# A macaron transformer layer on one core: the opening's transposes, norms and weight halves in another order

## The reference, cut to what matters

```
x = x + 0.5 * ffn(layernorm(x))          # W = dequant(q, scales, zeros) + lora; 512 x 512, and a bias
x = x + block(layernorm(x))              # below
x = x + 0.5 * ffn(layernorm(x))          # the same W

def block(h):                            # res = h
    h = res + mamba2(rmsnorm(h))         # w_in 512 -> 1284, causal conv of 4 taps, silu, scan by chunks of 128, w_out
    return h + mlp(rmsnorm(h))           # silu(gate) * up, 1792 wide, down
```

## Time and profile before

| | |
|---|---|
| median of 3 runs | 748.85 us (748.61 to 750.54) |
| the profiled execution | 749.22 us, its span 747.5 us |
| TensorE busy | 737.0 us, 99% of the span |
| VectorE busy | 637.2 us, 85% |
| ScalarE busy | 455.7 us, 61% |
| GpSimd busy | 341.5 us, 46% |

### The profile page before, as it was taken

How to read it: one execution, slowest core, us unless ns; L and a number is a source line. 1 busy time by engine, 2 the same in 40 slices (tenths; PEclk the granted TensorE clock), 3 DMA queues, 4 the chain that set the end, 5 groups by cost and what they waited for, 6 DMA issues and landing times.

```text
span 747.5 us, 10693 instructions
## 1 busy us (share of the span) xinstructions
PE 737.0 (99%) x3443; PEld 362.0 (48%) x3443; DVE 637.2 (85%) x1254; ACT 455.7 (61%) x895; POOL 341.5 (46%) x393
## 2 busy tenths in 40 slices
PE   9999999999999999989999999999999999999998
PEld 4454455555555565534444444444444444444444
DVE  7899999889989997977999977977977977767994
ACT  4977888687887777435446555456457356444441
POOL 5731446665453457896232153143243242214574
PEclk9999999999999999999999999999999999999999
DMA  8934646574431224320703635635634734434465
GB/s 301 217 76 82 163 96 126 121 134 100 100 85 43 44 71 121 77 84 1 170 14 60 153 59 99 153 57 94 159 57 85 168 58 77 78 71 84 114 169 141
DMA packets 98886, 77.83 MB, mean 104 GB/s; under 512 B 65616, under 2 KB 73104, under 8 KB 98832
## 3 DMA queue, kind: packets, MB, share of 16 engines
q0 software_dynamic: 17280, 31.46, 23.7%
q1 hardware_dynamic: 78640, 41.09, 21.3%
q10 hardware_dynamic: 2912, 4.61, 2.1%
HBM read 24.94 MB, written 5.54 MB: 41 GB/s over the span
## 4 chain that ended last, share of the span: by engine, by line
PE 73%; DVE 16%; ACT 4%; DMA 3%; issue 2%; POOL 1%; SPq 0%; ACTq 0%; DVEq 0%; POOLq 0%
PE PS L2285 61%; DVE stage L1672 2%; PE PS L2431 1%; DMA raw_d<-down_t 1%; PE PS L2423 1%; DVE st L1495 1%; PE PS L2389 1%; PE PS L2416 1%; PE PS L2420 1%; PE PS L2399 1%; DVE raw L1672 1%; PE PS L2407 1%; PE PS L2381 1%; PE PS L2529 1%; DVE h2n_p L1585 1%
## 5 line engine op out<-in xcount | busy, mean ns | idle before, releaser
L2285 PE MATMUL PS<-h,w_in 128*128 128x512 f16 (+1 forms) x504 | 108.1, 369 | 0.0
L2285 PE MATMUL PS<-h,x_t 128*128 128x512 f16 x408 | 95.5, 384 | 2.9 <-DMA h<-h2n_p 2.9
L784 POOL DMA_DIRECT2D xs<-x x42 | 36.7, 882 | 91.7 <-ACT x L1361 88.6
L2285 PEld LDWEIGHTS PS<-h,w_in 128*128 128x128 f16 x504 | 48.8, 98 | 59.9 <-issue 11.0
L2285 PE MATMUL PS<-n_T,stage 128*128 128x512 f16 x288 | 71.5, 379 | 0.0
L2285 PEld LDWEIGHTS PS<-h,x_t 128*128 128x128 f16 x408 | 39.7, 99 | 52.6 <-issue 4.5
L1361 ACT ACTIVATE x<-PS,d_d 128x512 f32<-128x512 f32 x59 | 40.3, 683 | 38.7 <-PE PS L2285 38.7
L584 POOL TENSOR_TENSOR r<-mv,mhalf 128x1 f32<-128x1 f32 (+1 forms) x32 | 29.0, 905 | 50.2 <-DVE mv L1499 36.4
L1331 ACT ACTIVATE xds<-tm,dgh 128x512 f32<-128x512 f32 x24 | 17.3, 722 | 53.4 <-DVE tm L2209 53.4
L2285 PE MATMUL PS<-pre,stage 128*128 128x512 f16 x192 | 49.3, 379 | 0.0
L2285 PEld LDWEIGHTS PS<-n_T,stage 128*128 128x128 f16 x288 | 28.1, 98 | 34.0 <-ACT x L1361 0.3
(11 more groups left out here) (346 smaller groups left out, 1880.6 us busy)
## 6 DMA issues: line engine op xcount, KB each, us to landing
xs<-x POOLq DMA_DIRECT2D x58, 256.0 KB, 3.3
xs<-n POOLq DMA_DIRECT2D x21, 256.0 KB, 3.3
xl<-x POOLq DMA_DIRECT2D x17, 256.0 KB, 3.3
x_t<-x_in SPq DMA_DIRECT2D x16, 256.0 KB, 4.0
x_t<-hb POOLq DMA_DIRECT2D x16, 256.0 KB, 4.8
out<-x_t SPq DMA_DIRECT2D x15, 256.0 KB, 2.3
raw_gu<-gate_t SPq DMA_DIRECT2D x7, 512.0 KB, 4.5
raw_gu<-up_t SPq DMA_DIRECT2D x7, 512.0 KB, 6.5
```

The source lines that it names most:

```text
L784: po.dma_start(end_row(c), d_tmps[d % 3], accum_op=ALU.add).then_inc(s_acc[d % 3], 16)
L2285: ins = pe.matmul(out_, lhs(a, b, k), rhs(a, b, k), start=first and n == 0, stop=last and n == len(todo) - 1)
```

## The change

On four engines the order of the opening is changed:

- TensorE: `first_f` can be done in parts. Block 4's transpose stands before the last of the four matmuls of block 3, block 5's behind the second of block 4; the transpose of the second maximum stands behind block 3's product, its spread behind the first matmul of block 4.
- ScalarE: `hi1` is two functions, the whole result (`hi1_whole`) and the high half (`hi1_high`). For blocks 1 and 2 the copy of a transposed block stands between them. `build_dw(0)` is ahead of `tc0(1)`, `w_in_sum(2)` ahead of `tc0(3)` and `hi1(0)`, and `hi1(3)` is behind the first piece of `w_in_hi`.
- VectorE: the low half of block 1 comes after block 5's statistics and the row of the maximum; `both_scales` before `x1_stats(3)`; `w_in_lo(0)` before the low half of block 3 and `x1_stats(4)`.
- GpSimd: `ln1_chain(2)`, `ln0(5)` and the bias DMA of block 4 stand before the selector `sel_f`.

```diff
@@ GpSimd
             ln1_chain(1, 1)
             ln0(4, 0)
+            ln1_chain(2, 2)
+            ln0(5, 1)
+            xb(4, 0)
             chain(po.memset(sel_f[:, :], 0.0))
...
-            ln1_chain(2, 2)
-            xb(4, 0)
             chain(po.tensor_copy(sel_b[:, :], sel_f[:, :]))
             po.sem_inc(e_const, 1)
-            ln0(5, 1)
             ln1_chain(3, 3)
@@ ScalarE
-                for dst in (hn_of(c), hn_parts(c)[:, 0, :]):
-                    last = ac.activation(dst, row(c), ACT.Identity, scale=r1[:, c, 1:2], bias=b1[:, c, 1:2])
-                last.then_inc(e_hn_hi, 1)
+                ac.activation(hn_of(c), row(c), ACT.Identity, scale=r1[:, c, 1:2], bias=b1[:, c, 1:2])
+
+            def hi1_high(c):
+                ac.activation(hn_parts(c)[:, 0, :], row(c), ACT.Identity, scale=r1[:, c, 1:2], bias=b1[:, c, 1:2]).then_inc(e_hn_hi, 1)
...
             hi0(1, 1)
-            tc0(1)
             ac.wait_ge(s_head, 48)
             ac.activation(a_neg[:, :], al[:, :], ACT.Exp).then_inc(e_aexp, 1)
             ac.wait_ge(e_tab, 2)
             build_dw(0)
+            tc0(1)
             hi0(2, 2)
...
             hi0(3, 3)
             w_in_sum(1)
+            w_in_sum(2)
             tc0(3)
             hi1(0, 0)
-            w_in_sum(2)
             w_in_sum(3)
-            hi1(1, 1)
             hi0(4, 0)
+            hi1_whole(1)
             tc0(4)
-            hi1(2, 2)
+            hi1_high(1)
             hi0(5, 1)
-            hi1(3, 3)
+            hi1_whole(2)
             tc0(5)
+            hi1_high(2)
             ac.wait_ge(e_scale, 1)
             w_in_hi(W_IN_PIECES[0])
+            hi1(3, 3)
             w_in_hi(W_IN_PIECES[1])
@@ VectorE
             x1_stats(2, 2, B_P[0])
             w_in_bound()
-            lo1(1, 1)
             prep0(5, 1)
             max_row(1)
+            lo1(1, 1)
+            both_scales()
             x1_stats(3, 3, B_P[1])
-            both_scales()
             lo1(2, 2)
+            w_in_lo(0)
             lo1(3, 3)
             x1_stats(4, 0, B_P[0])
-            w_in_lo(0)
             small_scales()
@@ TensorE
-            def first_f(c):
-                pe.wait_ge(e_n0T, c + 1)
-                if c - 1 > 0:
-                    pe.wait_ge(e_x1, c - 1)
-                for k in range(KB):
+            def first_f(c, k0=0, k1=KB):
+                if k0 == 0:
+                    pe.wait_ge(e_n0T, c + 1)
+                    if c - 1 > 0:
+                        pe.wait_ge(e_x1, c - 1)
+                for k in range(k0, k1):
...
-                last.then_inc(e_ffn, 1)
+                if k1 == KB:
+                    last.then_inc(e_ffn, 1)
...
             max_spread(0)
-            first_f(3)
+            first_f(3, 0, 3)
+            first_t0(4)
+            first_f(3, 3, KB)
             max_turn(1)
-            first_t0(4)
+            first_f(4, 0, 1)
             max_spread(1)
-            first_f(4)
+            first_f(4, 1, 2)
             first_t0(5)
+            first_f(4, 2, KB)
             first_f(5)
```

More of the change, by code:

```diff
@@ L844, in tc0, with hi1_whole @@
                 ac.activation(nT32[c % 2].rearrange("p k t -> p (k t)"), bank(B_TA), ACT.Copy).then_inc(e_n0T, 1)
-            def hi1(c, j):
+            def hi1_whole(c):
                 ac.wait_ge(e_hn_scale, c + 1)
@@ L855, in hi1 @@
                     ac.wait_ge(e_hn_lo, c - 1)
-                for dst in (hn_of(c), hn_parts(c)[:, 0, :]):
-                    last = ac.activation(dst, row(c), ACT.Identity, scale=r1[:, c, 1:2], bias=b1[:, c, 1:2])
-                last.then_inc(e_hn_hi, 1)
+                ac.activation(hn_of(c), row(c), ACT.Identity, scale=r1[:, c, 1:2], bias=b1[:, c, 1:2])
+            def hi1_high(c):
+                ac.activation(hn_parts(c)[:, 0, :], row(c), ACT.Identity, scale=r1[:, c, 1:2], bias=b1[:, c, 1:2]).then_inc(e_hn_hi, 1)
+            def hi1(c, j):
+                hi1_whole(c)
+                hi1_high(c)
             def hi2(c, j):
```

## The result

The changed kernel is slower: the median of 14 executions is 751.92 us (749.63 to 754.08) against 748.90 of 14 of the kernel before (748.61 to 750.54), a ratio of 1.0031 (95% interval 1.0024 to 1.0038). The forecast of 748.9 us, with 750.8 as its upper end and 0.90 on a difference under 0.3%, was wrong. The executions of the changed kernel are not spread evenly: six lie between 749.6 and 750.7, seven between 751.8 and 752.4, one at 754.1. So there are two things to explain: about 1 us that every execution lost, and about 2 us more in half of them.

A forecast was written before the change was run, and what follows sets the result against it. TensorE's gaps bound the opening, 1.4 us to be had, but lost to block 3's transpose and VectorE's late halves; VectorE's 1.0 lateness less 0.84 leaves 0.15. Sum +0.1: 748.85 + 0.1 = 748.9 us, range 747.2 to 750.8.

The forecast's parts named there:

- The three gaps: TensorE waits at the maximum's spread (0.50), before product 5 (0.69) and before the input product (0.22): 1.4 us together.
- the chain through TensorE to ScalarE's copy and the taps: Chain of waits leaves TensorE at 66.25 for a conv copy on ScalarE; VectorE's taps follow from 67.64.
- late for 0.84 us: VectorE sat idle 0.84 us before the taps at 67.64, so it may be that much later for nothing.
- ScalarE: ScalarE to 25 us: earlier identities, block 2's normalization and third sum; VectorE's first low half at 24.55, 0.35 us later.
- the transposes inside products: Products 3 and 4: TensorE waits 0.5, VectorE +0.6 for the maximum; 0.50 and 0.69 gaps go, product 5 ends 1.1 earlier.
- the scales: VectorE's scales, behind block 1's low half, wait for the maximum's spread, which ends at 31.1: +0.3 us on VectorE.
- the first halves: Input weights: ScalarE starts high halves at 33.8, VectorE waits 0.55, low halves ready at 37.2; the 0.22 gap goes.
- Row block 3: Late norm and DMA transpose, landing taken as 41.3 (40.7 to 41.9): new TensorE wait of 1.1 us near 40.2.
- the slow price of GpSimd: GpSimd's power in block 3's norm at 1.09 instead of 0.72 us: adds 0.4, making the sum +0.4, inside the range.
- The bias DMA: Block 4's bias DMA goes out about 1.4 us later; its reader moves by more, from 35.15 to 37.7.
- The clock: Rival, chance 0.07: TensorE's clock falls in the new wait, a loss of 1.8; taps 2.2 late, 751.1 us.
- Carried over: VectorE's 1.0 us lateness at 43 reaches the taps at 67.64 less its idle 0.84, leaving 0.15; TensorE without gain.

The follow-up runs named there:

- both changed profiles: The changed kernel as it is, profiled in each of two timings: executions of 750.65 and 751.88 us; medians 751.92 and 750.69.
- the scales moved back: Changed kernel with VectorE's `both_scales` behind the residual of block 3 again, as before the change: median 749.17 us, ratio 1.0005.
- The idle and the busy version of the kernel before: Kernel before, third half product on TensorE delayed by an added wait (median 751.1 us, ratio 1.0027) or by ten junk matmuls (751.32, 1.0031).
- the kernels with a shorter wait: Four kernels waiting 0.9 to 1.4 us for block 3: scales back 749.17, bias DMA sooner 749.63, both 749.78, first halves alone on kernel before 750.04.
- the two high executions with junk in the wait: Changed kernel with block 3's residual first on all engines, plus five junk matmuls in TensorE's wait: median 749.98 us, two executions at 753.3 and 751.1.
- both mends together: Changed kernel with `both_scales` behind block 3's residual and block 5's bias DMA ahead of block 3's second norm on GpSimd: median 749.78 us, ratio 1.0010.
- the changed kernel's second profile: The changed kernel timed once more, nothing altered: median 750.69 us, ratio 1.0025; the profiled execution took 751.88 us.
- block 3's residual first, without and with junk: Changed kernel reordered on four engines for block 3's residual: median 749.9 us, ratio 1.0011; with five junk matmuls in TensorE's wait: 749.98, 1.0015.

## Why the prediction was wrong

*What bounds the kernel: right.* The three gaps, 1.4 us at stake, and the chain through TensorE to ScalarE's copy and the taps. That VectorE could be late for 0.84 us was right too: in both changed profiles it still waited there.

*ScalarE, the transposes inside products, the scales, the first halves: right.* Without the late input of 0.66, block 4's transpose began at 28.1 (forecast 28.2), the input product at 37.7 (37.5). TensorE's wait before that transpose was 0.16 and not 0.5: the third matmul of product 3 ends at 27.9 and not at 27.7, since product 3 starts at 25.32 in the kernel before and three matmuls take 2.58. Of the waits foretold for VectorE, the one for the maximum was 0.30 and not 0.6, for the halves 0.59 (0.55), for block 3's norm 0.41 (0.1). VectorE's lateness at its second piece was 2.2 us, 1.6 without the late input, where I had 1.0; it lay behind TensorE's own and cost nothing.

*Row block 3: the mechanism right, the size wrong. This is the step that failed.* "I take 41.3" for its landing; it landed at 43.25, 42.6 without the late input, and the wait of 1.1 us was 2.26. The residual started where it was forecast (32.4, forecast 32.5). Two terms behind it were too small. GpSimd's pair took 1.09 + 0.53 us where the chain of 3.05 us had the quick price of 0.70 + 0.27: 0.65. From the end of the low half to the landing it was 4.2 us where I had 3.5 (37.8 to 41.3): 0.7. The prediction named the slow price of GpSimd and held it for a side case of 0.4. These are the power in the changed kernel and, below it, with the scales moved back:

```profile
35.02 1.09 POOL L584 TENSOR_TENSOR r<-mv,mhalf 128x2 f32<-128x2 f32 x1 [1.12 <-DVE mv L1506]
...
33.44 0.72 POOL L584 TENSOR_TENSOR r<-mv,mhalf 128x2 f32<-128x2 f32 x1 [0.18 <-POOL sel_b L663]
```

The first ran beside a low half with two SBUF inputs (VectorE, 34.85), the second began before it (33.91). The rule of the Trainium skill (SBUF — State Buffer, "Who interferes with whom") applies by its own words, and the trace agrees.

*The bias DMA: priced at nothing, on the wrong reader.* I asked whether the residual of block 5 would find it in time. It did. What it met was the transpose of block 3. In the kernel before it was issued at 33.14, 2.2 us ahead of that transpose, which took 3.9. I took less than 3.9 because block 3's transpose "would now have fewer beside it". But `xb(5)` waits behind `ln1_chain(3)`: when block 3's residual came late, the bias DMA was late with it (37.04) and again stood 2.0 us ahead. That is a DMA of a moved step, followed to its own reader and not to the other users of the DMA engines.

*The clock: the rival came true, its chance was too small.* I gave 0.07 that the clock falls in the new wait, with a decision point between 0.7 and 2.9 us. A wait of 2.3 us was enough in about half of the executions. The price of 1.8 was close: 1.6 measured on the products, and like for like the earlier trace rows gives 1.7, since 24 such matmuls take 5.35 us where the clock stays up (the first changed profile at 331.28); the 5.18 that I took counts from start to start. Since the wait's size was forecast with both ends at 0.5 and 1.7 us, the case seemed remote; with a wait of 2.3 it decides the median. The median of 751.92 is the 748.90 of before, about 1 for the late block, and about 2 for the clock (752.1 against 749.8 between the groups; of this the profile shows the 1.6, the rest it doesn't place). The late block alone would have stayed within the range, at 749.8.

*Carried over: right.* The idle and the busy version of the kernel before show that TensorE's lateness at 44 us reaches the end whole. VectorE's is carried less its 0.84 us, as the prediction had it, and shows in the kernels with a shorter wait.

What stays open: why equal waits of 2.26 and 2.27 us left the clock at 1.00 in one execution and at 0.50 in another, the two high executions with junk in the wait, and 0.3 to 0.4 us of the median of both mends together, which neither engine's lateness accounts for.

## What to carry to other kernels

Closing a gap on the bounding engine pays only if the next input is there, and mending that input's lateness pays only down to the next engine's; price that input's whole chain at the slow end of each row, since late steps meet neighbours that they didn't have before. When a wait of a few microseconds on TensorE may arise, count the clock in as likely, not as a remote case (behind waits of 2.2 to 2.9 us it fell in 11 of 18 cases here), and look at single executions, because the median jumps between two levels. Follow each DMA that a moved step issues to the other users of the DMA engines at its new time, not only to its reader.

## What the runs showed of the hardware

A DMA transpose of the same block (128 x 1024 of fp16) took from 2.9 to 4.7 us to land, and it goes with the accumulating bias DMA ahead of it. Issued 1.6 to 2.3 us after that DMA it took 3.7 to 4.7 us (4.2 in three profiles of the changed order); issued 2.9 to 5.9 us after it, 2.9 to 3.5. The distance isn't all: at the same 1.65 us it took 4.7 us in one profile and 3.7 in another (block 3's residual first, without and with junk), where the bias DMA itself took 5.5 and 4.4. In the six profiles of the changed kernel and its variants with a distance of 1.6 to 2.0 us, the transpose landed 0.6 to 1.0 us after the bias DMA had. In the changed kernel's second profile the DMA rate from 34 to 44 us, in steps of 0.25, shows the pattern:

```profile
GB/s 180 164 205 82 319 328 131 0 0 167 290 289 305 31 0 0 123 213 188 205 197 107 8 138 336 113 0 2 8 9 9 181 293 33 0 0 0 0 0 0
```

The transpose was issued at 38.61. One burst moves from about 39.75 to 40.5 (138, 336, 113), which is 0.15 MB; then the engines are all but idle for more than a microsecond (0 to 9), and a second burst moves from 41.75 to 42.5 (181, 293, 33), 0.13 MB. Together they come to about the block's 0.26 MB, so I read them as its two halves. So the time is not bandwidth. The bias DMA, issued at 36.59, landed at 42.2, between the start and the end of the second burst; whether the second half waits for it isn't shown.

TensorE's clock left 2.4 GHz after waits of 2.23, 2.27 and 2.29 us in profiles of three orders, and stayed after 2.26, 1.93, 1.42, 1.23, 1.10 and 0.94. At 329 us every profile has such a wait: it fell after 2.90, 2.64, 2.62, 2.56, 2.50, 2.46, 2.42 and 2.35, and stayed after 2.74, 2.68, 2.54, 2.37, 2.27 and 2.23. So between 2.2 and 2.9 us the length of the wait doesn't say whether it falls. The Trainium skill (TensorE: Matmul & The Clock Gate, "HAM oscillation — how this bites in real kernels") has the same fall behind waits for data; these profiles agree, and show that it may come in some executions of a kernel and not in others.
